# Where the small weight loads of a four-layer graph kernel are issued

## What is computed

```python
# layers 0 and 2: additive attention
Wh = x @ W
e = leaky_relu((Wh @ a[:64])[:, :, None] + (Wh @ a[64:])[:, None, :], 0.2)
out = elu(softmax(where(adj == 0, e - 1e9, e)) @ Wh)        # layer 2: masked with -9e15
# layer 1: attention per feature
feat = softplus(x * (w0 / sqrt(2)) + b0)
scores = feat * wa + ba
out = einsum("bijd,bjd->bid", softmax_over_j(mask(scores)), feat)
# layer 3: dot-product attention, four heads and then one
h = einsum("bnc,hdc->bhnd", x, Wh)
cat = concat_heads(softmax(mask(h @ h.T)) @ h + bh)
h2 = leaky_relu(cat) @ Wo.T
z = leaky_relu(softmax(mask(h2 @ h2.T)) @ h2 + bo)
out = layernorm(z) * gamma + beta
```

## Time and profile before

| | |
|---|---|
| median of the runs | 2091.6 us |
| the profiled execution's own time | 2092.67 us |
| its span, first to last instruction | 2090.9 us |
| mean granted TensorE clock | 0.959 |
| TensorE busy, matmul | 1913.1 us, 91% |
| VectorE busy | 1626.3 us, 78% |
| ScalarE busy | 1250.6 us, 60% |
| GpSimd busy | 587.9 us, 28% |

### The profile page before, as it was taken

How to read it: one execution, slowest core, us unless ns; L and a number is a source line. 1 busy time by engine, 2 the same in 40 slices (tenths; PEclk the granted TensorE clock), 3 DMA queues, 4 the chain that set the end, 5 groups by cost and what they waited for, 6 DMA issues and landing times.

```text
span 2090.9 us, 51901 instructions
## 1 busy us (share of the span) xinstructions
PE 1913.1 (91%) x22356; PEld 1186.8 (57%) x22356; DVE 1626.3 (78%) x1913; ACT 1250.6 (60%) x2298; POOL 587.9 (28%) x453
## 2 busy tenths in 40 slices
PE   6999759995999659999999999999999999999983
PEld 4888637774888534455455455455455554554543
DVE  3999828874999657787887887888888888878863
ACT  3677756652777636655656656656656656656552
POOL 0233238872223300021221311212212212212214
PEclk8999969997999879999999999999999999999996
DMA  6000000000000000001101001000011010010010
GB/s 162 3 4 3 3 1 1 1 1 2 4 3 3 2 5 20 24 12 37 27 12 37 21 17 37 22 17 27 13 36 27 12 37 27 12 37 27 12 38 20
DMA packets 50348, 42.20 MB, mean 20 GB/s; under 512 B 33096, under 2 KB 36744, under 8 KB 50120
## 3 DMA queue, kind: packets, MB, share of 16 engines
q1 hardware_dynamic: 50120, 38.89, 6.8%
HBM read 25.76 MB, written 4.72 MB: 15 GB/s over the span
## 4 chain that ended last, share of the span: by engine, by line
PE 57%; DVE 5%; POOL 1%; issue 1%; ACT 0%; DMA 0%; SPq 0%; ACTq 0%; POOLq 0%; DVEq 0%
PE fourth_ps_out L1378 21%; PE fourth_ps_scores L1330 7%; PE fourth_ps_out L1392 6%; PE fourth_ps_scores L1333 5%; PE fourth_ps_scores L1336 5%; DVE fourth_weights L1034 3%; PE fourth_ps_scores L1354 2%; PE fourth_ps_prep L1295 2%; PE fourth_ps_prep L1305 2%; PE fourth_ps_scores L1363 1%; PE fourth_ps_scores L1357 1%; PE fourth_ps_scores L1360 1%; PE fourth_ps_prep L1287 1%; PE fourth_ps_prep L1265 1%; DVE fourth_cat L1013 1%
## 5 line engine op out<-in xcount | busy, mean ns | idle before, releaser
L1034 DVE TENSOR_TENSOR fourth_weights<-fourth_weights,keep_mask 128x1024 f32<-128x1024 f32 x512 | 666.5, 1342 | 109.2 <-ACT fourth_weights L1183 107.2
L1183 ACT ACTIVATE fourth_weights<-fourth_ps_scores 128x1024 f32<-128x1024 f32 x512 | 497.3, 1024 | 357.9 <-PE fourth_ps_scores L1336 337.2
L1378 PE MATMUL fourth_ps_out<-fourth_weights,fourth_x_stage 128*64 128x512 f32 x2048 | 498.0, 605 | 4.4 <-DVE fourth_weights L1034 4.4
L1378 PEld LDWEIGHTS fourth_ps_out<-fourth_weights,fourth_x_stage 128*64 128x64 f32 x2048 | 124.3, 136 | 250.4 <-issue 217.1
L1330 PE MATMUL fourth_ps_scores<-fourth_g_high,fourth_x_high 64*128 64x512 f32 x1024 | 230.1, 446 | 2.6 <-DVE fourth_g_low L1001 2.4
L1330 PEld LDWEIGHTS fourth_ps_scores<-fourth_g_high,fourth_x_high 64*128 64x128 f32 x1024 | 96.2, 184 | 201.3 <-issue 101.4
L1333 PE MATMUL fourth_ps_scores<-fourth_g_high,fourth_x_low 64*128 64x512 f32 x1024 | 202.7, 392 | 0.0
L1336 PE MATMUL fourth_ps_scores<-fourth_g_low,fourth_x_high 64*128 64x512 f32 x1024 | 201.6, 390 | 0.0
L1190 ACT ACTIVATE fourth_weights<-fourth_ps_scores 128x1024 f32<-128x1024 f32 x128 | 125.2, 1026 | 113.3 <-PE fourth_ps_scores L1363 113.3
L1041 DVE TENSOR_TENSOR fourth_weights<-fourth_weights,keep_mask 128x1024 f32<-128x1024 f32 x128 | 153.1, 1237 | 43.3 <-ACT fourth_weights L1190 43.3
L434 DVE SCALAR_TENSOR_TENSOR first_weights<-first_ps_row,first_gain,keep_mask 128x1024 f32<-128x1024 f32 x128 | 159.3, 1267 | 2.5 <-ACT first_ps_row L535 2.5
(11 more groups left out here) (264 smaller groups left out, 3010.1 us busy)
## 6 DMA issues: line engine op xcount, KB each, us to landing
fourth_recip_wide<-recip_out SPq DMA_DIRECT2D x128, 128.0 KB, 3.0
setup_adj<-in_adj SPq DMA_DIRECT2D x8, 512.0 KB, 6.8
fourth_h_high<-fourth_h_high SPq DMA_DIRECT2D x32, 128.0 KB, 2.9
fourth_h_low<-fourth_h_low SPq DMA_DIRECT2D x32, 128.0 KB, 2.5
out<-keep_x SPq DMA_DIRECT2D x16, 256.0 KB, 2.6
dens_out<-fourth_mixture SPq DMA_DIRECT2D x64, 4.0 KB
keep_x<-in_x SPq DMA_DIRECT2D x1, 512.0 KB, 11.1
fourth_dens<-dens_out SPq DMA_DIRECT2D x32, 8.0 KB, 1.6
```

Source lines behind the costliest of these rows:

```text
L1034: dve.tensor_tensor(buf, buf, keep.mask[:, st.t, cols(half)].bitcast(F32).unsqueeze(1) .to_broadcast([P, 2, HALF]), ALU.mult).then_inc(wei ...
L1183: act.activation(weights[st.slot + half][:, :], ps_scores[half][:, :], ACT.Exp)\
L1378: last = pe.matmul(ps_out[rows(g), cols(half)], x_stage[st.s][:, st.t, g, :], weights[st.slot + half][:, cols(g)], start=(st.t == 0), stop ...
```

## The change

The 22 small loads are issued by SP in the opening stage, after the adjacency and the first x rows. The lines that issue them go from the lists of SP in the four layers' stages (in the diff below this is shown for the additive layers). Their tiles, and the semaphores that count them, become `keep` tiles and semaphores. The two additive layers have a set each. The waits of the engines on the loads stay where they are, on the new semaphores. SP's list of the first stage then holds only the load of x for batches 2 to 15, those of the second and third are empty, and that of the fourth begins with its loop. GpSimd's clearing of `bias_rows` moves to the opening stage, and both GpSimd and SP wait for it there. The short description of the change also speaks of "head products on the quarters of the array"; the diff has no line on a product.

```diff
@@ setup, SP
                 sp.dma_start(keep.x[:, 0:2, :, :], x_rows(ins)[:, 0:2, :, :]).then_inc(keep.first_x_loaded, 16)
+                for layer, (w_name, a_name) in enumerate((("L0_gnn_W", "L0_gnn_a"), ("L2_gnn_W", "L2_gnn_a"))):
+                    for half in range(2):
+                        sp.dma_start(keep.w[layer][half * DIM:(half + 1) * DIM, :], ins[w_name])\
+                          .then_inc(keep.additive_loaded[layer], 16)
+                    for k in range(2):
+                        sp.dma_start(keep.a_cols[layer][:, k:k + 1], ins[a_name][k * DIM:(k + 1) * DIM, :])\
+                          .then_inc(keep.additive_loaded[layer], 16)
+                sp.dma_start(keep.scalars[:, 0:1], ins["L1_gnn_w0"].to_broadcast([P, 1])).then_inc(keep.feature_loaded, 16)
...
+                sp.dma_start(keep.bias_col[:, :], ins["L1_gnn_ba"].unsqueeze(1)).then_inc(keep.feature_loaded, 16)
+                for g in range(2):
+                    sp.dma_start(keep.wh_in[:, g, :], ins["L3_gnn_Wh"][2 * g:2 * g + 2, :, :]
+                                 .rearrange("h d c -> (h d) c")).then_inc(keep.dot_loaded, 16)
+                sp.dma_start(keep.wo_in[:, :], ins["L3_gnn_Wo"]).then_inc(keep.dot_loaded, 16)
+                for k, name in enumerate(("L3_gnn_bo", "L3_gnn_gamma", "L3_gnn_beta")):
+                    sp.dma_start(keep.rows_in[:, k, :], ins[name].unsqueeze(0).to_broadcast([P, DIM]))\
+                      .then_inc(keep.dot_loaded, 16)
+                sp.wait_ge(keep.bias_cleared, 1)
+                for h in range(HEADS):
+                    at = (h % 2) * DIM
+                    sp.dma_start(keep.bias_rows[at:at + 1, h, :], ins["L3_gnn_bh"][h:h + 1, :])\
+                      .then_inc(keep.dot_loaded, 16)
@@ setup, GpSimd
                 pool.memset(row_used[:, :], 0.0).then_inc(consts, 1)
+                pool.memset(keep.bias_rows[:, :, :], 0.0).then_inc(keep.bias_cleared, 1)
+                pool.wait_ge(keep.bias_cleared, 1)
                 pool.wait_ge(consts, 6)
@@ additive_layer
-        w = sb("w", [P, DIM])
+        w, a_cols, loaded = keep.w[layer], keep.a_cols[layer], keep.additive_loaded[layer]
...
-                for half in range(2):
-                    sp.dma_start(w[half * DIM:(half + 1) * DIM, :], w_in).then_inc(loaded, 16)
-                for k in range(2):
-                    sp.dma_start(a_cols[:, k:k + 1], a_in[k * DIM:(k + 1) * DIM, :]).then_inc(loaded, 16)
                 if x_in is not None:
                     sp.dma_start(keep.x[:, 2:BATCH, :, :], x_in[:, 2:BATCH, :, :]).then_inc(keep.x_loaded, 16)
@@ dot_layer, GpSimd
-                pool.memset(bias_rows[:, :, :], 0.0).then_inc(bias_cleared, 1)
```

More of the change, by code:

```diff
@@ L271, in _, with additive_layer @@
                        .then_inc(copied, 1)
-def additive_layer(nc, stage, keep, w_in, a_in, x_in=None):
+def additive_layer(nc, stage, keep, layer, x_in=None):
     with ExitStack() as stack:
@@ L695, in dot_layer @@
         BUILT = TILES + 2 * HEADS + 3 * HEADS
-        wh_in = sb("wh_in", [P, 2, DIM])
+        wh_in, wo_in, rows_in, bias_rows = keep.wh_in, keep.wo_in, keep.rows_in, keep.bias_rows
+        loaded = keep.dot_loaded
         wh_twice = sb("wh_twice", [P, 2, 2, DIM])
-        bias_rows = sb("bias_rows", [P, HEADS, DIM])
         form_high = sb("form_high", [P, PAIRS, P], F32R)
@@ L1901, in build @@
         setup(nc, ins, keep)
-        additive_layer(nc, "first", keep, ins["L0_gnn_W"], ins["L0_gnn_a"], x_rows(ins))
+        additive_layer(nc, "first", keep, 0, x_rows(ins))
         feature_layer(nc, "second", keep, ins)
-        additive_layer(nc, "third", keep, ins["L2_gnn_W"], ins["L2_gnn_a"])
+        additive_layer(nc, "third", keep, 1)
         dot_layer(nc, "fourth", keep, ins, out)
```

52 lines of the change are left out of this document (23 added, 29 removed).

## The result

The changed kernel takes **2076.55 us** (median of 4 runs, 2073.28 to 2078.83), the kernel before 2092.12 us beside it (4 runs, 2090.79 to 2094.11). The ratio is 0.9924, with a 95% interval of 0.9906 to 0.9941. So it is faster, by 15.6 us where 20.3 were forecast; it lies inside the range, and 5.2 us above the predicted 2071.3 (4.7 us of gain are missing, and 0.5 is that the kernel before took 2092.12 us here and 2091.6 in the forecast). The profiled execution took 2076.72 us with a span of 2074.9, against 2092.67 and 2090.9: 16.0 us less from span to span. The mean granted clock is 0.960 after 0.959.

A forecast was written before the change was run, and what follows sets the result against it. Bound at the four stage starts by small loads landing behind the barrier. 0 + 4.7 + 4.5 + 4.1 + 7.0 = 20.3 us off the 2091.6 us median gives 2071.3 us; range 2067 to 2078.

The forecast's parts named there:

- The opening stage: 0 us: Opening stage: SP's 22 added loads, priced at 12.1 us, fit its 17.1 us wait and cost 0 us.
- the cover: Opening stage: SP's 17.1 us wait for the stage's end hides 12.1 us of issues, with 5.0 us left.
- my first rival: Opening stage: SP held behind the x rows until 15.7, barrier 5.6 us later, gain 14.7, time 2076.9 us; chance 8%.
- First stage, 4.7 predicted: First stage's start: 4.15 us from starting without the small loads, plus 0.5 us for the clock.
- The 0.5 for a clock still at full: First stage's start: first products run earlier, in the stretch still at 2.4 GHz, gaining 0.5 us.
- The load of x binds: First stage: the load of fourteen x batches limits the gain to 5.2 us; as full-clock rival 2070.8 us, no separate chance.
- Second stage, 4.5 predicted: Second stage's start: ScalarE's first activation moves from 278.49 to its table load's end at 273.98, gaining 4.5 us.
- Third stage, 4.1 predicted: Third stage's start: TensorE starts 0.05 us behind the barrier at 484.60 instead of at 488.75, gaining 4.1 us.
- cold before and after, so no clock term: Third stage's start: TensorE is cold before and after the change, so the clock adds 0 us.
- Fourth stage, 7.0 predicted: Fourth stage's start: VectorE starts 6.65 us earlier, subtractions shorten, GpSimd's copies may hold the masks; gain 7.0 us.
- the upper bound of 8.1: Fourth stage's start: gain of 8.1 us if GpSimd's copies do not hold up VectorE's masks.
- Nothing swallows the gain later: All four stages: each start is a serial chain behind a barrier, so the 20.3 us stay gained.

The follow-up runs named there:

- kernel 1: The changed kernel with the x rows of batches 0 and 1 issued behind the 22 small loads instead of ahead of them; 2073.67 us.
- kernel 2: The changed kernel with batch 0 of the x rows ahead of the small loads and batch 1 behind them; 2073.29 us.
- kernel 4: The changed kernel with the fourth stage's ten loads issued at that stage's start again, GpSimd's memset staying in the opening stage; 2081.17 us.
- kernel 5: kernel 1 with 20 extra products of 128 by 512 in TensorE's waits at the fourth stage's start; 2070.44 us.
- kernel 6: kernel 1 with GpSimd, in the first and third stages, waiting for VectorE's five copies before its memsets; 2072.63 us.

## Why the prediction was right, and where it was off

The sign and the range held; the forecast was too fast by 5.2 us. By its steps:

- **"The opening stage: 0 us" failed.** It took +2.35 us, of which 1.85 are SP's. The 12.1 us for 22 issues were about right (21 of them took from 13.3 to 24.26, 11.0 us; in kernel 1 all 22 took 11.6). What failed is the cover: the first of them was held 8.2 us behind the x rows. I had argued from SP's nine large loads, all issued by 5.1, that nothing holds SP; kernels 1 and 2 show that the hold comes with the next issue behind the x rows. That was my first rival, and it was right in its mechanism and too dear in its price: it let SP go at 15.7 and took 12.1 us from there, SP went at 13.3 and took 11.0, so the barrier moved by 2.35 us instead of 5.6. That its time, 2076.9, came out so near is chance: what the starts gave back with the clock, which the rival doesn't have, made up for most of the price that it had too high.
- **First stage, 4.7 predicted, 3.6 measured.** The start of 4.15 came as 3.8; the turn of x came 2.5 us behind the opening and not 2.1, with VectorE's copy 0.8 us longer beside GpSimd's memset: a collision I had not looked for, since I had checked only that the memsets end in time. The 0.5 for a clock still at full failed because the stage opened later, and the clock had fallen before (0.81 over 23 to 25). In kernel 1, which opened at 22.61, the clock was still full: there the turn came at 2.2 and took 0.86 us instead of 1.11, so 0.55 us sooner in all, but the stage was only 0.2 us shorter. The load of x binds nowhere: it left at 25.29 and landed 19.8 us later at 45.1, and the product that needs it ran at 47.04 without a wait.
- **Second stage, 4.5 predicted, 5.4 measured.** The start gave 4.5 as worked out; the other 0.85 is the clock's, as the same code at 206.55 to 207.69 us in the table shows.
- **Third stage, 4.1 predicted, 2.7 measured.** The start gave 3.7 (the copy again); "cold before and after, so no clock term" failed: 1.1 us went back because full clock came only 1.4 us sooner for work that was 3.7 us ahead. In kernels 2, 4 and 5 this stage gave nothing back, so the 1.1 is this trace's.
- **Fourth stage, 7.0 predicted, 6.7 measured**, by two errors that cancel. The start gave 8.3, a little over the upper bound of 8.1: I had taken 7.0 from a VectorE held by GpSimd's copies during the masks, and the masks ran at 1.69 us as before while GpSimd's two copies took 3.26 us instead of 1.99. Then 1.6 us went back. The clock came 2.7 us later for the work; that this alone is the 1.6 is not shown, since the same code took 1347.4 to 1350.3 us.
- "Nothing swallows the gain later" failed: 2.0 us net of all four stages went back here, and about 2 on average over four kernels. I had put the clock into the range as 2 us either way and into the sum at +0.5. That the sum of the starts, 20.3 us, equals the forecast is luck: the first and third gave less than I had put in, the fourth more.

The rule of the Trainium skill by which I had chosen between 7.0 and 8.1 (SBUF — State Buffer, "SBUF: two separate sides") says that when a GpSimd operation meets a VectorE operation that needs the shared ports too (in a mode with both ports, or with two SBUF inputs against a GpSimd operation that reads SBUF), the one that starts first gets them for its whole instruction and the other is blocked. I had used only one direction of it. This case's traces agree with both. VectorE is held in the first stage, where its copy took 1.03 us beside the memset and 0.21 without it in kernel 6. GpSimd is held in the fourth: the masks run from 725.76 to 727.45, and GpSimd's first copy, started at 726.05 among them, took 2290 ns where the next took 1024. The 1.27 us more is about the 1.40 us that the masks had left. So the step that failed is which engine waits. The eight masks are instructions of their own, and why GpSimd got no turn between two of them is open.

Left open: why SP is held for 8.2 us behind 512 KB and 5.1 behind 256. No run changed the size of the pieces or of the small loads. Nor was it tried whether issues of the small loads ahead of the adjacency rows would be free.

## What to carry to other kernels

When loads move to an earlier place, look at what stands ahead of them in the same queue, not only at how long the issuing engine idles there: 17 us of idle time were not enough for 12 us of issues behind one transfer of 512 KB, and behind all the small loads that transfer cost nothing. Small loads that stand alone behind a barrier are worth moving even so; ten of them paid about 9 us for 1.6. A start that is shortened can give part back through TensorE's clock, here about 2 of 20 us on average. Products that nobody reads, put into TensorE's waits behind an opening, brought full clock 15 us sooner in the fourth stage and 5 in the first; in the fourth they were worth 3 us. And before a microsecond of one stage is explained, look at the same stage in other runs of the same code: here it differed by 1 to 3 us by itself.

## What the hardware showed that I had not expected

- The issue of a 16 KB load took 8157 ns on SP with 512 KB of x rows ahead of it in its queue, 5125 ns with 256 KB, and 567 to 597 ns with none. With the same rows in ScalarE's queue it was not held.
- 512 KB of x rows that move among the 4 MB of adjacency rows delay the last of these by 2.8 us (13.54 to 16.35).
- A VectorE copy of 64 by 128 took 1.03 us beside a GpSimd memset of 0.52 and 0.21 us without it, while the eight masks of 128 by 128 kept their 1.69 us beside GpSimd's two copies of x, which grew from 1.99 to 3.26 because the first of them started among the masks.
- With the same code and in different runs, full clock came 17.8 to 21.1 us behind the third stage's opening and 19.1 to 21.8 behind the second's, and the stage was 0.4 to 0.5 us longer for each us that it came later.
- 226 products that brought the granted clock to 1.00 at three openings gained nothing that the runs show (2070.37 us with them, 2069.19 without), and 20 in the waits behind an opening gained 3.2 us.
